# Thirty-two graph blocks on one Trainium2 core: partition-first host arrays, new instruction orders for the first and last graphs, and the gate's shift as a minimum

## What is computed

```
x = norm(x + relu([x, (adj @ x) / deg] @ W0))                      # deg: row sums of adj
x = norm(x + gcn3(gcn2(gcn1(x))))                                  # gcn: adj @ (x @ W) + b, relu on two
x = norm(x + attention(x, mask, adj) @ W_out + b_out)              # 8 heads of 64
    # attention weights: 0.33 * softmax(q k / 8, masked) + 0.33 * adj + 0.33 * exp(-adj)
x = norm(x + w * (x @ W_v)),  w = softmax over nodes of sum_m (q_n . k_m / 8) * adj[n, m]
```

## Time and profile before

| | us |
|---|---|
| three runs | 1298.72, 1299.63, 1299.93 |
| median | 1299.63 |
| the profiled execution, its own time | 1296.4 |
| its span, first to last instruction | 1294.6 |
| TensorE busy in the span | 1276.8 (99%) |
| VectorE busy | 1198.8 (93%) |
| ScalarE busy | 912.2 (70%) |
| GpSimd busy | 139.7 (11%) |
| granted TensorE clock, mean | 0.999 |

### The profile page before, as it was taken

One profiled execution on the slowest core, in us unless ns is written; L12 is line 12 of the kernel. 1 busy time (PEld: TensorE's weight loads), 2 busy tenths in 40 slices (PEclk: granted clock), 3 DMA queues, 4 the chain that ended last, 5 costly groups with the idle time before them and its releaser, 6 DMA issues.

```text
span 1294.6 us, 30579 instructions
## 1 busy us (share of the span) xinstructions
PE 1276.8 (99%) x10987; PEld 1173.4 (91%) x10987; DVE 1198.8 (93%) x3821; ACT 912.2 (70%) x2445; POOL 139.7 (11%) x265
## 2 busy tenths in 40 slices
PE   8999999999999999999999999999999999999997
PEld 7899999999999999999999999999999999999985
DVE  6898999999999999999999999999999999998996
ACT  6677767677667677677677676776676776776773
POOL 0000110101110101111101101011101011110011
PEclk9999999999999999999999999999999999999999
DMA  5211011110111110111100111101111101110000
GB/s 193 68 35 35 1 44 43 43 43 2 43 43 43 43 36 8 43 43 43 43 20 25 44 43 43 43 2 43 43 43 43 35 10 43 43 43 10 9 10 25
DMA packets 51588, 49.03 MB, mean 38 GB/s; under 512 B 7920, under 2 KB 51184, under 8 KB 51440
## 3 DMA queue, kind: packets, MB, share of 16 engines
q1 hardware_dynamic: 51440, 47.08, 11.7%
HBM read 38.68 MB, written 8.39 MB: 36 GB/s over the span
## 4 chain that ended last, share of the span: by engine, by line
PE 96%; DVE 1%; ACT 1%; DMA 1%; issue 0%; POOL 0%; SPq 0%; POOLq 0%; DVEq 0%; ACTq 0%
PE psum L1478 63%; PE psum L1492 13%; PE psum L1722 9%; PE psum L1684 8%; PE psum L1773 1%; PE psum L1776 1%; DMA adj_sb<-in_adj 1%; PE psum L1785 1%; PE psum L1795 0%; POOL rstd L338 0%; ACT fT_h L378 0%; DVE bn L859 0%; SPq L238 0%; DVE x L893 0%; ACT adj_junk L434 0%
## 5 line engine op out<-in xcount | busy, mean ns | idle before, releaser
L526 ACT ACTIVATE work<-work,shift 128x256 f32<-128x256 f32 x512 | 253.6, 499 | 35.9 <-DVE shift L1022 35.9
L1041 DVE SCALAR_TENSOR_TENSOR work<-work,rsum,extra 128x256 f32<-128x256 f32 x512 | 216.4, 472 | 0.2
L378 ACT ACTIVATE work<-psum 128x512 f32<-128x512 f32 x256 | 138.2, 595 | 76.1 <-PE psum L1492 72.2
L1022 DVE CUSTOM_DVE_ANT_0 work<-psum,minus_big 128x256 f32<-128x256 f32 x512 | 189.3, 415 | 0.7 <-PE psum L1684 0.7
L378 ACT ACTIVATE sup_h<-psum 128x512 fp32r<-128x512 f32 x128 | 75.9, 593 | 148.0 <-PE psum L1478 148.0
L335 POOL TENSOR_TENSOR mv<-mv,eps 128x2 f32<-128x2 f32 x128 | 33.0, 258 | 1140.8 <-DVE mv L880 1140.8
L1478 PE MATMUL psum<-x2T_h,wqkv_h 128*128 128x256 f32 x512 | 145.3, 284 | 0.0
L1478 PE MATMUL psum<-x2T_l,wqkv_h 128*128 128x256 f32 x512 | 142.2, 278 | 0.0
L1478 PE MATMUL psum<-x2T_h,wqkv_l 128*128 128x256 f32 x512 | 142.1, 278 | 0.0
L1492 PE MATMUL psum<-ident,work 128*128 128x128 f32 x1024 | 129.3, 274 | 0.0
L1722 PE MATMUL psum<-work,v_sb 128*64 128x256 f32 x1024 | 124.6, 385 | 0.0
(11 more groups left out here) (134 smaller groups left out, 3735.2 us busy)
## 6 DMA issues: line engine op xcount, KB each, us to landing
xT_sb<-in_xT SPq DMA_DIRECT2D x32, 256.0 KB, 2.8
adjT_sb<-in_adjT SPq DMA_DIRECT2D x32, 256.0 KB, 3.2
adj_sb<-in_adj SPq DMA_DIRECT2D x32, 256.0 KB, 4.7
x_sb<-in_x SPq DMA_DIRECT2D x32, 256.0 KB, 4.9
out<-y_sb SPq DMA_DIRECT2D x32, 256.0 KB, 4.6
work<-in_L_gnn_W_qkv SPq DMA_DIRECT2D x1, 1536.0 KB, 9.6
mask_row<-in_nodemask SPq DMA_DIRECT2D x32, 32.0 KB, 4.6
w_raw<-in_L_gnn_W SPq DMA_DIRECT2D x3, 256.0 KB, 6.7
```

Of the source, the lines that this page charges most:

```text
L378: return nc.scalar.activation(dst, src, ACT.Copy, scale=scale)
L526: last = nc.scalar.activation(prob[:, p % 2, i, h], prob[:, p % 2, i, h], ACT.Exp, bias=shift[:, p % 2, h, i:i + 1], scale=-1.0, accum_out ...
L1022: last = V_.tensor_tensor_reduce(out=prob[:, p % 2, i, h], in0=bank(SCORES[p] + h)[:, i * N:(i + 1) * N], in1=minus_big[:, g % 2, i], scal ...
L1041: last = V_.scalar_tensor_tensor(out=prob[:, p % 2, i, h], in0=prob[:, p % 2, i, h], scalar=rsum[:, p % 2, h, i:i + 1], in1=extra[:, g % 2 ...
```

## The change

Host arrays. x, adj, xT, adjT and all weights are brought on the host into a shape with the partition in front (`by_partition`), so that the bytes of one partition lie together in HBM: 2 KB instead of two rows of 1 KB for each matrix of a graph. W0 becomes two halves and W1, W2, W3 one array. The output keeps its layout. The loads, their order on SP and their sizes are as before.

The gate. `tail_gate` uses a negative scale, and gives the negated scores. `gate_maximum` takes a minimum of their row, which is the shift itself; the second instruction (L1090) is gone, and `gate_exps` uses scale -1.

Orders. ScalarE, VectorE and TensorE get new orders in `first_graphs` and `last_graphs`. `slot(s)` is unchanged on all engines. GpSimd and SP are unchanged. Some waits are dropped, some added, some swapped within a helper.

```diff
-    by_node = "g (n p) f -> g p n f"
-    x_d, adj_d, out_d = (a.rearrange(by_node, p=P) for a in (x, adj, out))
-    xT_d, adjT_d = (a.rearrange(by_node, p=P) for a in (xT, adjT_in))
+    out_d = out.rearrange("g (n p) f -> g p n f", p=P)
...
-                sp.dma_start(w0_raw[:, :, cols], w0_d[:, :, cols]).then_inc(dma_w0[half], 16)
+                sp.dma_start(w0_raw[:, :, (1 - half) * F:(2 - half) * F], w0_d[half]).then_inc(dma_w0[half], 16)
...
+    def by_partition(a):
+        return a.reshape(a.shape[:-2] + (-1, 128, a.shape[-1])).swapaxes(-3, -2)
+    inputs["xT"] = by_partition(inputs["x"].transpose(0, 2, 1))
...
@@ ScalarE, helpers
-                if g == 4:
-                    reuse(act, pe_sup[0], once(g - 1))
-                else:
-                    reuse(act, pe_self, once(g - 1))
+                reuse(act, pe_self, once(g - 1))
...
                 act.wait_ge(dma_adjT[g % 2], loaded(g))
+                reuse(act, pe_adjk, once(g - 4))
                 copy(adjT[0][:, g % ADJS], adjT_sb[:, g % 2]).then_inc(act_adjT, 1)
...
                 nc.scalar.activation(gate_exp[:, :], bank(GATE_ROW)[0:1, 0:N], ACT.Exp, bias=gate_shift[:, :],
-                                     accum_out=gate_sum[:, :]).then_inc(act_gate_exp, 1)
+                                     scale=-1.0, accum_out=gate_sum[:, :]).then_inc(act_gate_exp, 1)
@@ ScalarE, first_graphs
                 sup0_hi(0)
+                x_hi(1)
                 degrees(0)
-                x_hi(1)
                 self_copy(0)
+                w123_hi(0)
                 adj_exp(0)
                 adj_hi(1)
-                w123_hi(0)
+                mask_bias(0)
+                self_copy(1)
+                sup0_hi(1)
+                degrees(1)
+                x1_hi(0)
+                sup_hi(0, 0)
                 w123_hi(1)
                 w123_hi(2)
-                sup0_hi(1)
-                self_copy(1)
-                x1_hi(0)
-                degrees(1)
-                sup_hi(0, 0)
                 hidden(0, 0)
                 hidden_hi(0, 0)
+                wqkv_hi(0)
                 sup_hi(1, 0)
-                wqkv_hi(0)
                 hidden(1, 0)
                 hidden_hi(1, 0)
-                wqkv_hi(1)
                 sup_hi(2, 0)
                 x1_hi(1)
-                mask_bias(0)
-                mask_bias(1)
+                wqkv_hi(1)
+                wout_hi()
                 adj_exp(1)
-                wout_hi()
                 sup_hi(0, 1)
-                degrees(2)
                 x_hi(2)
-                adj_hi(2)
                 hidden(0, 1)
                 hidden_hi(0, 1)
                 x2_hi(0)
+                w3_hi()
+                adj_hi(2)
                 sup_hi(1, 1)
+                degrees(2)
...
                 exps(0, 1, 1)
-                w3_hi()
+                mask_bias(1)
...
                 sup_hi(0, 2)
+                adj_hi(3)
...
+                sup_hi(1, 2)
+                x_hi(3)
+                mask_bias(2)
@@ VectorE
-                V_.tensor_reduce(gate_max[:, :], bank(GATE_ROW)[0:1, 0:N], AX.X, ALU.max).then_inc(dve_gate_max, 1)
-                dve.wait_ge(dve_gate_max, once(g))
-                V_.tensor_scalar(gate_shift[:, :], gate_max[:, :], -1.0, None, ALU.mult).then_inc(dve_gate_shift, 1)
+                V_.tensor_reduce(gate_shift[:, :], bank(GATE_ROW)[0:1, 0:N], AX.X, ALU.min).then_inc(dve_gate_shift, 1)
@@ VectorE, first_graphs
+                w0_lo(0)
                 x_lo(0)
-                w0_lo(0)
...
                 sup_lo(0, 0)
-                aggregate(1)
+                adj_extra(0)
                 w123_lo(1)
...
                 norm_apply(0, 1)
-                adj_extra(0)
                 hidden_lo(1, 0)
...
                 sup_lo(0, 1)
+                x_lo(2)
                 norm_apply(1, 0)
-                x_lo(2)
-                adj_sum(1)
+                wout_lo()
                 hidden_lo(0, 1)
                 x2_lo(0)
+                adj_sum(1)
+                adj_lo(2)
+                x1_bias(1)
                 adj_extra(1)
-                adj_lo(2)
-                degrees(2)
-                wout_lo()
+                x2_bias(0)
                 sup_lo(1, 1)
                 qk_lo(0, 0)
                 qk_lo(0, 1)
-                x1_bias(1)
                 scores(0, 0, 0)
@@ VectorE, last_graphs
                 tail_k(G - 2)
+                x2_bias(G - 1)
+                norm_mean(3, G - 3)
                 out_lo(G - 1, 0)
...
                 out_lo(G - 1, 3)
-                x2_bias(G - 1)
                 gate_maximum(G - 2)
@@ TensorE, waits
             def x1_transpose(g):
-                if g == 0:
-                    pe.wait_ge(act_self, once(g + 1))
                 pe.wait_ge(dve_x[0], once(g))
...
             def x2_transpose(g):
                 pe.wait_ge(dve_x[1], once(g))
-                pe.wait_ge(dve_agg, once(g + 1))
...
             def qk(g, p):
-                if p in (2, 3):
+                if p == 2:
                     reuse(pe, act_oT, nth(g - 1, p))
                     reuse(pe, dve_oT, nth(g - 1, p))
-                if p == 3:
-                    pe.wait_ge(dve_sup0, once(g + 2))
-                    pe.wait_ge(act_sup0, once(g + 2))
...
             def scores(g, p):
+                if p == 1:
+                    reuse(pe, dve_oT, nth(g - 1, p))
                 if p == 2:
+                    reuse(pe, act_gate_col, once(g - 2))
                     reuse(pe, dve_x3_pre, once(g - 1))
@@ TensorE, first_graphs
                 support0(1, HI)
+                support0(1, LO)
                 self_product(1)
-                support0(1, LO)
-                keep_busy(7, 3)
+                keep_busy(7, 7)
                 aggregate(1, HI)
...
                 values(0, LO)
+                aggregate(2, HI)
+                aggregate(2, LO)
                 qk(0, 2)
                 qk(0, 3)
-                aggregate(2, HI)
-                aggregate(2, LO)
```

More of the change, by code:

```diff
@@ L11, with graph_blocks_kernel @@
 AX = mybir.AxisListType
[L14 to L16 removed]
+def graph_blocks_kernel(nc, x_d, adj_d, nodemask, xT_d, adjT_d, w0_d, w123_d, L1_b1, L1_b2, L1_b3, wqkv_d, wout_d,
+                        L2_bout, w3_d, out):
+    G, N, F = out.shape
     P = 128
@@ L735, in first_graphs @@
                 probs_t(1, 3, 1)
-                adj_exp(4)
-                out_hi(1, 2)
-                gate_exps(0)
-                out_hi(1, 3)
-                exps(2, 0, 0)
-                sup_hi(1, 3)
-                qk_hi(2, 2)
-                exps(2, 0, 1)
-                mask_bias(3)
-                adj_hi(4)
-                hidden(1, 3)
-                exps(2, 1, 0)
+                out_hi(1, 2)
+                out_hi(1, 3)
+                x_hi(4)
+                exps(2, 0, 0)
+                gate_exps(0)
+                sup_hi(1, 3)
+                exps(2, 0, 1)
+                exps(2, 1, 0)
+                exps(2, 1, 1)
+                qk_hi(2, 2)
+                hidden(1, 3)
+                self_copy(4)
+                adj_exp(4)
                 hidden_hi(1, 3)
-                degrees(4)
-                exps(2, 1, 1)
                 sup_hi(2, 3)
                 sup0_hi(4)
-                self_copy(4)
                 values(2)
                 qk_hi(2, 3)
+                probs_t(2, 0, 0)
                 gate_column(0)
-                probs_t(2, 0, 0)
                 probs_t(2, 0, 1)
@@ L1324, in last_graphs @@
                 scores(G - 3, 3, 1)
+                x2_bias(G - 2)
                 x3_lo(G - 4)
-                x1_bias(G - 1)
+                norm_stats(3, G - 5)
                 x1_lo(G - 1)
                 out_lo(G - 3, 0)
+                qk_lo(G - 2, 0)
+                norm_mean(3, G - 5)
+                sup_lo(0, G - 1)
                 recip_sums(G - 3, 2)
+                tail_k(G - 4)
+                probs(G - 3, 2, 0)
                 recip_sums(G - 3, 3)
-                probs(G - 3, 2, 0)
@@ L1346, in last_graphs @@
+                hidden_lo(0, G - 1)
+                out_lo(G - 3, 2)
                 gate_maximum(G - 4)
-                out_lo(G - 3, 2)
+                norm_apply(3, G - 5)
+                sup_lo(1, G - 1)
+                scores(G - 2, 1, 1)
                 out_lo(G - 3, 3)
-                scores(G - 2, 1, 0)
-                scores(G - 2, 1, 1)
-                sup_lo(1, G - 1)
+                x1_bias(G - 1)
+                qk_lo(G - 2, 2)
+                gate_probs(G - 4)
+                adj_extra(G - 1)
```

297 lines of the change are left out of this document (142 added, 155 removed).

## The result

The kernel after takes 1295.53 us (median of 10 runs, 1295.19 to 1297.30). The kernel before, run beside it, took 1297.61 (10 runs, 1295.98 to 1300.66); the ratio is 0.9981, 95% interval 0.9972 to 0.9990, so the change makes it faster by 2.5 us (1.3 to 3.6). The interval excludes no change, and the gain is just under the 0.2% (2.6 us) that the prediction had drawn as its line. In a later comparison on another occasion the same two kernels gave 0.9971 (0.9960 to 0.9983), 3.8 us. The forecast was 1296.8, a gain of 2.8 on the median of 1299.63; against that median the gain is 4.1. But the two *profiled* executions, on which the sum was built, are only 1.0 us apart: 1295.42 after, 1296.4 before. Both differences want an explanation, and they are not the same one.

What follows compares the result with a forecast made beforehand. TensorE, busy 99% of the span, was taken as the bound. Gains of 2.2 (hole) + 0.2 (start) + 0.18 (negation) + 0.2 (last graphs) = 2.8 us off 1299.63 gave 1296.8, range 1295.3 to 1299.0.

Steps and rivals of the forecast that it cites:

- Part 1, the hole: TensorE's idle time before support0(2,HI), near 38 us: issuing load(2) near 22 us gains 2.2 us, bounds 0 and 2.3.
- rival (a): A new wait, in hidden(1,1,LO) and scores(0,0), takes part of the hole: gain 1.6, time 1298.0; chance 0.25.
- Part 2, the start: First 36 us: 2 KB pieces land W0's first half sooner and move the chain up 0.2 us, bounds -0.1 and 0.6.
- If the chain before 36 us came later: Sign of a wrong forecast: the start of the chain before 36 us comes later than in the kernel before.
- The rule of the Trainium skill: DMA pieces of 512 B already reach line rate; by it the layout term would be 0, the sum 0.2 smaller.
- Part 3, the end: Last graph's gate: without the negation 0.18 us go; changed operator and scale cost nothing, bounds 0 and 0.05.
- The new order of the last graphs: Near 1188 us: may save the loader's 0.2 us wait for hidT_l; taken 0.2, bounds -0.5 and 0.5.
- Part 4, waits: In the slots: dropped waits had long been met, added ones are met in time; cost 0.
- rival (d): Slower: a new wait binds in each slot, at scores(g,2) behind the gate's column; 1301.5 us; chance 0.05.
- The step from the profile to the median: Median of runs lies 3.2 us above the profiled 1296.4; the 2.8 us gain was taken unchanged off 1299.63.
- rival (c): The start gains more: W0, x and adjT land 0.5 us or more earlier; gain 4, time 1295.6; chance 0.07.

Runs made afterwards that it cites:

- b_load2: Kernel before with mask_bias(0) behind adj_hi(1), x_hi(2) ahead of degrees(2), adj_extra(0) behind sup_lo(0,0); median 1295.33 us, ratio 0.9974; b_load2_again is its second profiling.
- a_again: Kernel after, unchanged, run and profiled again beside other kernels; median 1295.74 us in 6 runs.
- a_deg: Kernel after with degrees(0) put back ahead of x_hi(1) on ScalarE and ahead of x_lo(1) on VectorE; median 1295.36 us, ratio 0.9973.
- a_rows: Kernel after with the arrays laid out in rows again (1 KB pieces), all orders kept; median 1295.68 us, ratio 0.9979.
- b_again: Kernel before, unchanged, run for a second profile; 1299.03 us.
- b_third: Kernel before, unchanged, run for a third profile; 1301.14 us.
- b_fill_again: Second profile of the kernel before with 11 filler transposes on TensorE between hidden(0,1,LO) and support0(2,HI); 1300.09 us.

## Why the prediction was right or wrong

**Part 1, the hole: right.** 2.2 us forecast, 2.26 measured from the start of `hidden(0,1)` to `qk(0,0)`. `load(2)` went out at 22.67 (forecast about 22), `support0(2,HI)` started with no idle time at 38.60 (38.19 in the walk, and 0.43 for the later start), and no wait over 0.2 us took its place on TensorE; rival (a) did not come. b_load2 shows it alone. Of these 2.26, 0.27 went until 65 us (0.14 in a_again) in waits under 0.1 us each, which I can't name one by one. The first `scores` on VectorE came at 47.20 where 46.6 was forecast; 0.43 of that is the start.

**Part 2, the start: wrong, in sign.** I forecast 0.2 us earlier; it was 0.43 later in the profile, of which 0.28 is the luck of the first profile of before (36.67, median of seven 36.95) and 0.15 is left. W0's first half took 3.5 us to land, not under 3.2. Not the size of the layout's term failed: in the old order of ScalarE it is worth 0.3 at `aggregate(0)`, though not by the landing of W0's first half, which I had named and which came later. What failed is the sentence that this moves the whole chain of the first 36 us up, and it failed because I had not walked `x_hi(1)` in its new place. It waits for `self_product(0)`, 0.82 us in after, and holds `degrees(0)` and `self_copy(0)` up behind it, 0.8 us at `aggregate(0)`; a_deg undid it and had `hidden(0,1)` 0.65 us earlier, at 36.45. "If the chain before 36 us came later" was written down as a sign of being wrong, and it was.

The rule of the Trainium skill cited there ("DMA: Bandwidth & Descriptors", Specifications: line rate from 512 B on) holds for the kernel after, where a_rows is as fast. The landing that the kernel before waits for is another matter, since a time to land is not a rate: graph 2's adj took 3.39, 4.25 and 4.31 us in 2 KB pieces, and 4.70 to 6.35 in the six profiles with 1 KB pieces. These are few, but they don't overlap.

**Part 3, the end: right in what was computed.** The 0.18 us of the negation came (0.19 measured). The new order of the last graphs gave 0.1 of the 0.2 forecast. What I costed at nothing was that 32 instructions fewer shift the places in VectorE's list at which its supply falls short.

**Part 4, waits: right for the waits, wrong as a sum.** No wait on `act_gate_col` shows in the slots, and rival (d) did not come. But "cost 0" for the slots should have been 0.65.

Together, in the profiled executions: 2.26 - 0.43 - 0.27 - 0.16 (to 99 us) - 0.07 - 0.68 (the two steps, with the 0.02 around them) + 0.1 + 0.18 = 0.93 against 2.8 forecast and 1.0 measured. The 0.16 is no loss of the change: b_load2_again, b_again and b_third show the same 0.19 there, so the first profile of before was lucky by it.

**The step from the profile to the median: wrong, and the largest.** I wrote that the median was 3.2 us above the profiled execution and that "the change works on the same instructions in both". The 3.2 us lay in the stretch that the change takes out: a longer landing and a halved clock behind it. The profiled run was of the third of the runs below 1298 us; the two profiles of before in that group had neither. So the gain in the median was 4.1 us from the 1299.63 given, although the profiles differ by 1.0. The 1299.63 was itself chance in part: it is the median of three runs, and the median of all 77 is 1298.87. The median after, 1295.53, stands 0.1 us above its profiled run, where I had left 3.2. The measured time lies inside the range by luck, because two errors of opposite sign met: 1.8 us too much in the sum, 3.1 us too little in the step to the median. With the step alone put right the forecast would have been 1293.7, 1.8 below what was measured. Even so 1295.53 is outside the forecast's own range of 2.2 to 3.4 us of gain; it lies next to the 1295.6 of rival (c), whose reason, earlier landings at the start, did not come.

## What to carry to other kernels

Where one profile stands for many runs, ask which wait in it could be longer in another run, above all a DMA landing that TensorE waits for with nothing to do: its price is the landing's spread and the clock behind it, and removing it gains more than the idle time in a good profile. A sum from one profile should be moved to the median only by what lies outside the stretches that the change touches. Of a reordered start, walk every operation past its wait, not only those that the change seems to be about.

## What the runs showed of the hardware

The same DMA of 256 KB, issued third of five at the same place, landed after 4.70, 4.88, 5.08 and 6.35 us in four runs of one kernel. After an idle time of 2.26 (b_again), 2.34 (b_fill_again) and 3.62 us (b_third) TensorE's granted clock read 0.50 for 3.4, 3.4 and 6.8 us; in b_again and b_fill_again this began only when TensorE had been at work again for 1.1 and 1.4 us, so the low stretch was paid in full. After 1.91 and 2.15 us it did not fall; these few profiles don't say what decides between them. In the first microseconds the matmuls of 128x256 can be 0.21 us apart while the clock column reads 1.00 (the first five in after's first profile, the first eight in b_again's). The trace's clock record begins only at 7.70 and 8.08 us there, just where the distance goes to 0.117, and the column reads 1.00 where there is no record; so at the start go by the distance of the matmuls. And one kernel's instruction supply falls short at the same instructions in every profile, so that removing instructions from VectorE, an engine that is not the bottleneck, cost TensorE 0.65 us.
